# A decoder in one kernel: the feed-forward part with its gate product two tiles ahead, the turned tile copied a step later, and doubled level and scale-row buffers

## What is computed

```
def bit_linear(x, w, b):
    gamma_x = clip(max(abs(x), axis=-1), 1e-5)
    x_dq = clip(round(x * 127 / gamma_x), -128, 127) * gamma_x / 127
    gamma_w = clip(mean(abs(w)), 1e-5)
    w_dq = clip(round(w / gamma_w), -1, 1) * gamma_w
    return x_dq @ w_dq.T + b
gate = silu(bit_linear(x, gate_w, gate_b))      # 256 -> 1024
val = bit_linear(x, val_w, val_b)               # 256 -> 1024
return bit_linear(gate * val, out_w, out_b)     # 1024 -> 256
```

## Time and profile before

| | |
|---|---|
| median of 3 runs | 1343.65 us (1343.45 to 1346.59) |
| time of the profiled execution | 1344.83 us |
| span of its instructions | 1343.0 us |
| PE busy, of the span | 1098.8 us |
| DVE busy | 867.2 us |
| ACT busy | 629.6 us |
| POOL busy | 318.8 us |

### The profile page before, as it was taken

How to read it: one execution, slowest core, us unless ns; L and a number is a source line. 1 busy time by engine, 2 the same in 40 slices (tenths; PEclk the granted TensorE clock), 3 DMA queues, 4 the chain that set the end, 5 groups by cost and what they waited for, 6 DMA issues and landing times.

```text
span 1343.0 us, 22126 instructions
## 1 busy us (share of the span) xinstructions
PE 1098.8 (82%) x6352; PEld 722.9 (54%) x6353; DVE 867.2 (65%) x2396; ACT 629.6 (47%) x1971; POOL 318.8 (24%) x465
## 2 busy tenths in 40 slices
PE   3677777789898779999999999999999999543690
PEld 2443444566666444556656566565665666332580
DVE  4676665687778747868677686776867675152252
ACT  1435766455555416555464555645555464021230
POOL 1213231131112313213132231322313110013334
PEclk9855999999999979899999999999999999855795
DMA  9401000122111000000000000000000000331455
GB/s 312 160 0 32 0 1 0 48 66 78 47 47 51 13 1 1 1 1 1 1 1 1 1 0 0 1 0 1 1 0 1 0 1 1 121 130 46 131 122 141
DMA packets 42436, 52.42 MB, mean 39 GB/s; under 512 B 4080, under 2 KB 34672, under 8 KB 42096
## 3 DMA queue, kind: packets, MB, share of 16 engines
q1 hardware_dynamic: 36464, 43.11, 10.2%
q10 hardware_dynamic: 4352, 4.20, 1.6%
q0 software_dynamic: 1536, 4.20, 1.0%
HBM read 34.71 MB, written 16.78 MB: 38 GB/s over the span
## 4 chain that ended last, share of the span: by engine, by line
PE 43%; issue 8%; DVE 5%; ACT 4%; POOL 1%; DMA 1%; SPq 1%; ACTq 1%; DVEq 0%; POOLq 0%
PE PS L1481 38%; PE PS L1825 2%; PE PS L1807 2%; ACT arena L1349 1%; ACT arena L1358 1%; POOL arena L1134 1%; DVE early L865 1%; DVE arena L725 1%; DVE arena L689 1%; ACT early L1291 1%; DVE arena L713 1%; ACT arena L1465 0%; SPq L945 0%; ACTq L1456 0%; DVE early L619 0%
## 5 line engine op out<-in xcount | busy, mean ns | idle before, releaser
L1481 PE MATMUL PS<-EW,arena 128*64 (+4 forms) x896 | 174.3, 333 | 18.8 <-DVE small L713 9.0
L1481 PEld LDWEIGHTS PS<-EW,arena 128*128 128x128 f32 (+1 forms) x896 | 125.4, 158 | 62.1 <-issue 42.5
L1481 PE MATMUL PS<-wq,EW 128*128 128x512 f32 x256 | 127.5, 621 | 6.9 <-DVE arena L689 6.8
L1481 PE MATMUL PS<-early,arena 128*32 128x128 f32 (+6 forms) x864 | 105.7, 359 | 33.2 <-DVE early L576 23.7
L1083 POOL TENSOR_SCALAR small<-small 128x4 f32<-128x4 f32 x64 | 26.2, 410 | 437.8 <-ACT mask L1342 363.7
L713 DVE CUSTOM_DVE_ANT_0 arena<-PS,kmask 128x128 f32<-128x128 f32 (+3 forms) x256 | 91.6, 382 | 51.3 <-PE PS L1481 45.9
L1358 ACT ACTIVATE arena<-arena,small 128x128 f32<-128x128 f32 (+3 forms) x256 | 119.4, 470 | 0.2
L1481 PE MATMUL PS<-wo,early 128*128 128x256 f32 x512 | 114.8, 382 | 0.8 <-ACT early L1372 0.8
L1349 ACT ACTIVATE arena<-PS 128x512 f32<-128x512 f32 x64 | 38.3, 598 | 161.3 <-PE PS L1807 161.3
L1481 PEld LDWEIGHTS PS<-wo,early 128*128 128x128 f32 x512 | 96.0, 190 | 18.5 <-issue 6.1
L985 POOL TENSOR_SCALAR ve<-mv 128x2 f32<-128x2 f32 x48 | 10.6, 221 | 370.5 <-DVE mv L348 370.5
(11 more groups left out here) (245 smaller groups left out, 2347.8 us busy)
## 6 DMA issues: line engine op xcount, KB each, us to landing
EW<-in_masksT_dram SPq DMA_DIRECT2D x32, 256.0 KB, 3.5
results_dram<-EW SPq DMA_DIRECT2D x32, 128.0 KB, 3.2
EW<-results_dram SPq DMA_DIRECT2D x4, 1024.0 KB, 9.6
rows_dram<-cosT SPq DMA_DIRECT2D x1, 4096.0 KB, 19.9
arena<-rows_dram SPq DMA_DIRECT2D x16, 256.0 KB, 3.1
results_dram<-early ACTq DMA_DIRECT2D x16, 256.0 KB, 3.2
X<-in_x_dram SPq DMA_DIRECT2D x1, 2048.0 KB, 9.3
wq<-in_wq_dram SPq DMA_DIRECT2D x1, 2048.0 KB, 11.0
```

Of the source, the lines that this page charges most:

```text
L1481: return pe.matmul(dst, lhs, rhs, start=first, stop=last)
```

## The change

Nothing is computed differently, and the only new instructions are waits. What moves:

- `level_turn` is split: `row_turn` transposes the two `cR` tiles into the unused half of bank 7, `level_turn` keeps the four level tiles, in bank 0. `levels` is split likewise into `rows` and `levels`. `cXT`, `cRT` and `c_so` get a slot for each parity.
- PE: before, each step wrote gate(u+1), down(u-1), value(u+1), turn(u). Now it writes value(u+1), gate(u+2), turn(u), down(u-1). The levels of batch b + 2 are turned at the end of batch b's second step, where before those of batch b + 1 were turned in its first.
- ACT: `evict` of the tile before comes behind `quantised`, where it headed the step. `applied(b + 2)` moves from the second step of batch b into its first, ahead of `quantised(b, 0)`. `rounded` and `rows` of batch b + 2 end the second step.
- DVE: `narrow` runs one step later and behind `prepare`. The ternary weights `ew` and three constants of the self attention are computed ahead of the first tile, where they followed the last.

```diff
-        cXQ = cut(0, (J, D)); cR = cut(512, (J, P)); cXT = cut(768, (C, S), BF); cRT = cut(1024, (S,), BF)
-        cHS = cut(1152, (HID,)); cH = cut(2176, (2, HID)); cHR = cut(4224, (HID,)); cHT = cut(5248, (HC, P), BF)
-        c_gx = small[:, 8:10]; c_sx = small[:, 12:14]; c_hm = small[:, 22:23]; c_sh = small[:, 24:26]; c_so = small[:, 26:28]
+        cXQ = cut(0, (J, D)); cR = cut(512, (J, P)); cXT = cut(768, (2, C, S), BF); cRT = cut(1280, (2, S), BF)
+        cHS = cut(1536, (HID,)); cH = cut(2560, (2, HID)); cHR = cut(4608, (HID,)); cHT = cut(5632, (HC, P), BF)
+        c_gx = small[:, 8:10]; c_sx = small[:, 12:14]; c_hm = small[:, 22:23]; c_sh = small[:, 24:26]; c_so = small[:, 26:30].rearrange("p (a j) -> p a j", a=2)
...
@@ -509,43 +510,43 @@
...
                     widen(b, j, par)
-                    step_size(b, j)
+                    step_size(b, j, par)
                     if j == 0 and left == 2:
                         ln_stats(FFN, b + 2)
                     if j == 0 and left == 0:
                         ln_stats(SELF, 0)
-                    if j == 1:
-                        narrow(b, 0)
-                    elif type(b) is not int or b > 0:
-                        narrow(b - 1, 1)
                     if j == 1 and left == 2:
                         prepare(b + 2, par)
+                    if type(b) is not int or b > 0:
+                        narrow(b - 1, j, 1 - par)
                     if j == 1 and left == 0:
                         ln_apply(SELF, 0)
 
             prepare(1, 1)
-            over_parities(dve, ffn)
-            narrow(B - 1, J - 1, 1)
-
             dve.wait_ge(s_l5, 64)
             ternary(ew[:, :, :], ew[:, :, :], 2.0)
             mark["ew"] = count[0]
-
             dve.wait_ge(s_l3, 16 * 7)
+            const(dve.tensor_reduce(d_half, hmask[:, :].rearrange("p (a e) -> p e a", e=2), AX.X, ALU.add))
+            const(dve.tensor_scalar(d_bq, bqk[:, 0:2], 0.25, None, ALU.mult))
+            const(dve.tensor_copy(d_mask, causal[:, 0, 0:P]), "self")
+            over_parities(dve, ffn)
+            narrow(B - 1, 0, 1)
+            narrow(B - 1, 1, 1, 1)
...
@@ -666,9 +667,6 @@
...
-            const(dve.tensor_reduce(d_half, hmask[:, :].rearrange("p (a e) -> p e a", e=2), AX.X, ALU.add))
-            const(dve.tensor_scalar(d_bq, bqk[:, 0:2], 0.25, None, ALU.mult))
-            const(dve.tensor_copy(d_mask, causal[:, 0, 0:P]), "self")
             self_keys(0, 0)
...
-                held(pool, s_xtp, FFN * B + b)
+                held(pool, c_rt, b)
...
-            def levels(b):
+            def rows(b, par):
+
+                act.wait_ge(c_rt, b + 1)
+                after(act, c_v, 2 * b - 2)
+                act.activation(cRT[:, par, :], PS[:, 7, D:D + S], ACT.Copy).then_inc(c_rc, 1)
+
+            def levels(b, par):
 
                 act.wait_ge(s_xtp, FFN * B + b + 1)
-                after(act, c_v, 2 * b)
-                act.activation(cXT.rearrange("p c s -> p (c s)"), bank(5), ACT.Identity, bias=unmagic[:, 0:1])
-                act.activation(cRT, PS[:, 6, 0:S], ACT.Copy).then_inc(s_xt, 1)
+                after(act, c_v, 2 * b - 2)
+                act.activation(cXT[:, par].rearrange("p c s -> p (c s)"), bank(0), ACT.Identity, bias=unmagic[:, 0:1])\
+                    .then_inc(s_xt, 1)
...
             def ffn(b, par, left):
                 for j in range(J):
-                    if j == 1:
-                        evict(b, 0)
-                    elif type(b) is not int or b > 0:
-                        evict(b - 1, 1)
-                    if j == 0 and left > 0:
-                        rounded(b + 1)
                     if j == 0:
                         gated(b, 1, par)
                     elif left > 0:
                         gated(b + 1, 0, 1 - par)
                     if j == 0 and left > 0:
-                        levels(b + 1)
-                    if j == 1 and left == 2:
+                        levels(b + 1, 1 - par)
+                    if j == 0 and left == 2:
                         applied(b + 2)
                     quantised(b, j)
+                    if j == 1:
+                        evict(b, 0)
+                    elif type(b) is not int or b > 0:
+                        evict(b - 1, 1)
+                    if j == 1 and left == 2:
+                        rows(b + 2, par)
+                        rounded(b + 2)
                     if j == 1 and left == 0:
                         xt_copy((SELF, 0))
 
-            levels(0)
+            rows(0, 0)
+            levels(0, 0)
             applied(1)
             gated(0, 0, 0)
+            rows(1, 1)
+            rounded(1)
             over_parities(act, ffn)
             evict(B - 1, 1)
             act.wait_ge(s_l3, 16 * 7)
@@ -1491,18 +1499,24 @@
                         last = pe.transpose(PS[:, to, at:at + P], XN[:, j, c * P:(c + 1) * P], ident[:, :])
...
+            def row_turn(b):
+
+                pe.wait_ge(c_r, b + 2)
+                after(pe, c_rc, b)
+                if type(b) is not int or b > 2:
+                    pe.wait_ge(s_x, FFN * B + b - 2)
+                for j in range(J):
+                    last = pe.transpose(PS[:, 7, D + j * P:D + (j + 1) * P], cR[:, j, :], ident[:, :])
+                last.then_inc(c_rt, 1)
+
             def level_turn(b):
 
                 pe.wait_ge(s_xn, FFN * B + b + 1)
-                pe.wait_ge(c_r, b + 2)
                 pe.wait_ge(s_xt, FFN * B + b)
-                after(pe, c_ht, 2 * b - 2)
-                for j in range(J):
-                    pe.transpose(PS[:, 6, j * P:(j + 1) * P], cR[:, j, :], ident[:, :])
                 for c in range(C):
                     for j in range(J):
                         at = c * S + j * P
-                        last = pe.transpose(PS[:, 5, at:at + P], cXQ[:, j, c * P:(c + 1) * P], ident[:, :])
+                        last = pe.transpose(PS[:, 0, at:at + P], cXQ[:, j, c * P:(c + 1) * P], ident[:, :])
                 last.then_inc(s_xtp, 1)
...
-            def gate(b, j):
+            def gate(b, j, par):
                 u = J * b + j
                 pe.wait_ge(s_xt, FFN * B + b + 1)
                 after(pe, c_si, u)
-                widen(1, gateT, 0, j).then_inc(c_g, 1)
-
-            def value(b, j):
+                widen(1, gateT, 0, j, par).then_inc(c_g, 1)
+
+            def value(b, j, par):
                 u = J * b + j
                 after(pe, c_h, u)
-                widen(3, valT, 2, j).then_inc(c_v, 1)
...
-            def turn(b, j, mixed):
+                widen(3, valT, 2, j, par).then_inc(c_v, 1)
+
+            def turn(b, j):
                 u = J * b + j
                 after(pe, c_ht, u)
-                if mixed:
-                    pe.wait_ge(s_xt, FFN * B + b + 2)
                 pe.wait_ge(c_hr, u + 1)
...
-            def down(b, j, at=7):
+            def down(b, j, at=7, mixed=False):
                 pe.wait_ge(c_ht, J * b + j + 1)
-                if j == 1:
+                if mixed:
+                    pe.wait_ge(c_rc, b + 3)
+                if at == 7 and j == 1:
                     pe.wait_ge(c_y, b + 1)
-                elif type(b) is not int or b > 0:
+                elif at == 7 and (type(b) is not int or b > 0):
                     pe.wait_ge(s_x, FFN * B + b)
...
@@ -1624,31 +1639,35 @@
             def ffn(b, par, left):
                 for j in range(J):
                     if j == 0:
-                        gate(b, 1)
+                        value(b, 1, par)
                     elif left > 0:
-                        gate(b + 1, 0)
+                        value(b + 1, 0, 1 - par)
+                    if left > 0:
+                        gate(b + 1, j, 1 - par)
+                    if j == 1 and left == 2:
+                        row_turn(b + 2)
+                    turn(b, j)
                     if j == 1:
-                        down(b, 0)
+                        down(b, 0, 7, left == 2)
                     elif type(b) is not int or b > 0:
                         down(b - 1, 1)
-                    if j == 0:
-                        value(b, 1)
-                    elif left > 0:
-                        value(b + 1, 0)
-                    if j == 0 and left > 0:
-                        level_turn(b + 1)
-                    turn(b, j, j == 0 and left > 0)
+                    if j == 1 and left == 2:
+                        level_turn(b + 2)
 
             pe.wait_ge(s_tern, 3 * B)
             pe.wait_ge(s_c, mark["bias"])
-            gate(0, 0)
+            gate(0, 0, 0)
             pe.wait_ge(s_x, FFN * B)
-            value(0, 0)
+            value(0, 0, 0)
+            row_turn(1)
+            level_turn(1)
+            gate(0, 1, 0)
             over_parities(pe, ffn)
             xt_turn(SELF, 0)
             pe.wait_ge(c_si, J * B)
             down(B - 1, 1, 1)
             pe.wait_ge(s_l3, 16 * 7)
+            pe.wait_ge(c_y, B)
             project(0, 0, d_pq)
```

(22 more changed lines are left out.)

## The result

| | before | changed |
|---|---|---|
| median | 1346.11 us (15 runs, 1343.45 to 1349.09) | 1351.21 us (15 runs, 1345.53 to 1352.47) |
| ratio | | 1.0036, 95% interval 1.0026 to 1.0046 |
| span of the profiled execution | 1343.0 us | 1349.9 us |

The changed kernel is slower by 0.36%, about 5 us. Forecast were 1338 us and a faster kernel; the time lies outside the range of 1330 to 1346. In the changed kernel `turn` is L1624, the plain matmuls L1489, row and level turns L1509 and L1519, `gated` L1242, `quantised` L1248, `evict` L1234, `levels` L1199, `applied` L1175, `widen` L502, the reciprocal L514, `narrow` L521, `self_queries` L1284.

What follows compares the result with a forecast made beforehand. No engine is full, so the order of waits bounds the kernel; 1.0 us at the start, 4.8 in the loops and 0.5 at the end give 6.3 us less, hence 1338 us, range 1330 to 1346.

Steps and rivals of the forecast that it cites:

- the loop: Feed-forward batches, reciprocal to reciprocal: quantised waits behind the moved applied for its statistics; 12.60 us a batch against 13.25.
- the sum: Feed-forward phase: savings of 1.0 us at the start, 4.8 in five loops, 0.5 at the end, 6.3 together.
- I assume no such fall after: Five loops: TensorE's granted clock would not drop to 0.50, as in one batch before, which cost 1.4 us.
- rival (a): First turns: clock falls in most batches, 1.4 to 3.1 us each, giving 1346.9 to 1357 us; chance 0.17.
- The pause itself: PE ahead of each batch's first turn: the wait grows from 2.35 to 2.9 us.
- The start: Phase start: the moved constants cost nothing; reciprocal (0,0) to (1,0) takes 10.7 us against 11.67, 1.0 less.
- The end: Last batches, reciprocal (6,0) to self_queries: no statistics chain, 24.6 us against 25.1, 0.5 less.
- (b): Second tile of each batch: its waits also close a loop, batch stays near 13.25 us, 1341.9 us; chance 0.10.
- (c): ACT at applied: POOL's chain doesn't hold it up, loops 1.3 us shorter, 1332 us or 1324 at PE's floor; chance 0.07.

Runs made afterwards that it cites:

- the filled version: Changed kernel with twelve unused matmuls of 512 columns ahead of the first turn of each batch with left = 2: 1340.22 us, ratio 0.9955 to before.
- `applied` behind: Changed kernel with applied(b+2) placed behind quantised(b,0) and evict(b-1,1) in ACT's queue: 1329.59 us, ratio 0.9880 to before.
- the two edits together: Changed kernel with applied(b+2) behind the eviction and, at the phase's start, gate(0,1) ahead of level_turn(1): 1324.15 us, ratio 0.9846 to before.

## Why the prediction was wrong

**What bounds the kernel, and the loop: right.** The step that named the moved `applied` as the new loop was right, link by link: reciprocal to turn 6.5 forecast, 6.55 measured; a loop of 12.60 forecast, 12.7 measured when the clock stays up (the filled version). So was the remark that the moved `applied` eats most of what the new order could give: the batch falls to 10.5 us once the wait is out of the way.

**The step that failed** is half a sentence of the sum: "I assume no such fall after". The five loops were put at 63.0 us at full clock and took 73.85; 10.2 us of that is the clock, and 0.65 the loop itself. The rival (a) had the mechanism and its prices (1.4 to 3.1 us a fall; measured 1.5 to 2.8; it counted six batches, and five had the pause), but I gave it 0.17, and for a bad reason: that the pause grows by 0.55 us only, and that six of seven pauses of 2.35 brought no fall. That took the count at one length as the chance at another. Measured, over the first turns of the batches (those of the changed kernel and its variants from batch 1 to 5, those of before from batch 0 on), and, in the last two rows, over the other pauses of 2.3 to 2.4 us in this phase:

| version | pauses ahead of the first turn | falls |
|---|---|---|
| before | 2.27 to 2.35 | 1 of 7 |
| changed, four products in the pause | 1.83, then 2.33 to 2.36 | 2 of 5 |
| changed | 2.12, then 3.28 to 3.32 | 5 of 5 |
| before, `applied` moved alone | 3.44 to 4.21 | 6 of 6 |
| changed, twelve products; changed, `applied` behind | 0.36 to 0.64 | 0 of 10 |
| before, eight products, and before, `applied` moved alone: first turn of batch 6 | 2.27 | 2 of 2 |
| changed and its six variants: last turn of the phase | 2.41 | 4 of 7 |

The version with the constants back repeats the row of the changed kernel (2.13, then 3.29 to 3.62, 5 of 5). From 2.35 to 3.3 us the falls go from three of eleven (2.27 to 2.36 in the first two rows) to all. With the last two rows it is nine of twenty pauses of 2.27 to 2.41 us, so that over these traces such a pause brought a fall nearly every second time; the one in seven of the single trace of before was too few to go by. (Where `applied` is moved alone, the clock falls at the end of that turn: 1.18 us, then 0.51 over the products behind it.) The one pause of 2.12 brought a fall too; no length can be read from the table below which there is none. The pause itself was sized 2.9 and came out at 3.3, since PE's run of products ended 0.3 to 0.4 us sooner than my sum of 9.7 had it (at 3.3 in the next batch instead of 3.6). Even 2.9 lay outside what the trace had shown to be mostly harmless, so the range should have held the slow end of rival (a).

**The start: right for the constants, wrong by 1.0 us for the loop.** The ternary weights and the constants ran from 127.63 to 129.62 and ended ahead of `widen(0,0)` at 130.41, as forecast, and their move is worth 0.7 us at the end. But (0,0) to (1,0) took 11.72 and not 10.7. PE's timeline, and ACT's behind it:

```profile
132.33 1.12 PE L1519 MATMUL PS<-ident,arena 128*128 128x128 f32 x4 [1.45 <-ACT arena L1185]
133.24 5.88 PE L1489 MATMUL PS<-early,arena 128*128 128x512 bf16 x18
...
135.73 1.11 ACT L1242 ACTIVATE arena<-PS,small 128x1024 f32<-128x1024 f32 x1 [3.46 <-PE PS L1489]
```

The level turn ahead of gate(0,1) makes PE wait for 1.45 us, and the clock, which in the kernel before rose during the first unbroken run of products, came up only in the run from 133.24 on: those 18 products took 5.88 us, where 18 at full clock take 4.0 (12 take 2.64). So the path here was another than the forecast's: ACT waited 3.46 us for the product of gate(0,1), and `levels`, `applied` and `quantised` followed it without a pause. The statistics did not hold it up.

**The end: wrong by 1.0 us, and that is the clock again.** 25.62 and not 24.6. The last turn of the phase, after and in the version with twelve products, which adds none at the end:

```profile
235.82 1.46 PE L1624 MATMUL PS<-ident,arena 128*128 128x128 f32 x8 [2.41 <-ACT arena L1234]
...
226.13 1.09 PE L1624 MATMUL PS<-ident,arena 128*128 128x128 f32 x8 [2.41 <-ACT arena L1234]
```

From the last reciprocal to `self_queries` the three profiled executions without this fall (twelve products, four products, and the two edits together) take 9.55 or 9.56 us, and that of the changed kernel 11.16. So this fall costs 1.6 us, and at full clock the whole stretch takes 24.0, less than the forecast's 24.6.

Added up: between the gain of 6.3 us that the sum had and the 6.9 us by which the span grew lie 10.85 in the loops, 1.0 each at the start and the end, and 0.7 ahead of the first reciprocal, less 0.3 behind the phase.

**Rivals (b) and (c).** The second tile's waits closed no loop: its turn follows without a pause (187.54). POOL's chain did hold ACT up, by 1.64 us in the batch shown.

## What to carry to other kernels

An engine's pause has two prices: its length, and on TensorE what the clock does behind it; where an edit lengthens a pause, the second can exceed everything that the edit saves. The one trace of before, with its shorter pauses, showed too few falls to price it. When other engines wait for an instruction, look at what stands ahead of it in its queue: here two small instructions waited there for a chain that starts only when the instruction's own input is complete, and moving them behind their neighbours turned 0.4% slower into 1.2% faster. To tell the clock from the waits, fill the pause with work that nobody uses. If the kernel gets faster with more work, while the instruction that ended the pause starts as late as before, it was the clock.

## What the hardware showed that I had not expected

Unused matmuls made the kernel faster: 12 products of 512 columns in each batch that has the pause brought 11 us. With the pause at 3.3 us the granted clock was at 0.50 behind every one of the four in the profiled execution, and with 2.34 us behind two in another, between pauses of 2.33 and 2.36 without a fall. A fall costs between 1.5 and 2.8 us in these loops, because the low level lasts through a part of the work behind it that differs from one to the next. The Trainium skill, *TensorE: Matmul & The Clock Gate*, Part 1, says that idle time takes the clock to half rate and that sustained work brings it back; the rows of batches 1 to 5 of the changed kernel agree with that: 0.50 in or right behind each first turn, 1.00 again at the second (1.04 us). The eleven pauses of 2.27 to 2.41 us without a fall show that not every idle stretch does it.
